# Wide attention of a decoder: causal mask moved from TensorE to VectorE, row sums to ScalarE, and a new order of TensorE's products

## The chip, the cores and the metric

One core of a Trainium2 chip runs the whole kernel as one program. The metric is the time of the program on the device in microseconds (us). Engines are called as the profile calls them: PE is TensorE's matmul, PEld its weight load, DVE is VectorE, ACT is ScalarE, POOL is GpSimd, SP is the queue that issues plain DMAs.

## The reference, cut to what matters

The program is a two-layer decoder on 64 sequences of 64 tokens with 128 channels. Narrow attentions and a mixture of experts come first; the change lies in the self-attention of the second layer, which has 16 heads of 64 dimensions:

```python
def _L1_attn_ref(x, Wq, Wk, Wv, Wo, bo):      # x: layer norm of the residual
    ...
    q = apply_rope(split_heads(x @ Wq))       # x1*cos - x2*sin, x1*sin + x2*cos
    k = apply_rope(split_heads(x @ Wk))
    v = split_heads(x @ Wv)
    sim = jnp.einsum('bid,bjd->bij', q, k) * scale          # scale = 64 ** -0.5
    sim = jnp.where(causal[None], sim, -jnp.inf)
    attn = jax.nn.softmax(sim, axis=-1)
    out = jnp.einsum('bij,bjd->bid', attn, v)
    ...                                       # heads side by side, then @ Wo + bo
```

## The kernel before, in words

The phase `wide_attention_phase` works on 16 blocks of 256 tokens (2 units of 128 rows, 4 sequences) and on 4 groups of 4 heads within each block: 64 items. An item n is a pair of block and group. Every engine has its own program, written as a prologue, a `step` of one block that loops over its 4 groups, and an epilogue; the engines meet at semaphores only, and each takes its instructions strictly in the order in which its program lists them. So that order is the schedule.

In step n PE does, in this order: scores of item n+1 (`scores`, L1540), transposes of the weights of item n (`transpose_e`, L1564), Q of item n+3 (`project_q`), V of item n+1 (`project_v`), K of item n+3 (`project_k`), in the first step of a block the transposes of the next block's input (`transpose_x`), output product of item n-1 (`project_o`), value products of item n (`weigh_values`, L1572). The causal mask is put in by PE: 8 bf16 matmuls (L1552) of an identity with a table of 0 and -1e30 open each bank of scores, and the 64 products of queries and keys (L1560) add to it.

Behind the scores DVE takes the maximum of each row (8 rows of 64 keys on each partition, L1789), subtracts it (L1793), and ACT makes one exponential of all 512 columns (L1674). DVE then adds up the rows (L1799) and takes reciprocals (L1804), POOL multiplies by them (L1440), PE transposes, ACT copies the transposed weights to SBUF (L1681), and PE multiplies with V. Between these, DVE multiplies Q and K by cos and sin (L1765, four operations of 512 columns per item), POOL adds and subtracts them (L1419, L1420), ACT copies V (L1670) and the value products (L1688).

PSUM has 8 banks: V and Q one each (the value products of an item go over both), one that K and the transposed weights share, one for the output, four for the scores. A second kind of work rides along once for each block: DVE adds the experts' rows to the residual (L1737, in the steps of groups 0 and 1), takes statistics (group 2) and centres (group 3), and adds the attention's result (L1810, group 1); ACT normalises (L1645), copies the block's transposed input (L1661) and keeps it (L1654); POOL gathers the experts' rows by DMA (L1456).

Of the kernel before, what the change touches and what calls it, by code (L numbers as in the profile page):

```python
# [7 lines left out]
P = 128  # L8
B, T, C = 64, 64, 128
# [1281 lines left out]
def wide_attention_phase(nc, k):  # L1291
# [11 lines left out]
    with ExitStack() as ctx:  # L1303
# [17 lines left out]
        sin = sb("sin", [P, T])  # L1321
        stats = sb("stats", [P, UB, 6])
# [15 lines left out]
        row_max = sb("row_max", [P, 2, GH * UB])  # L1338
        row_sum = sb("row_sum", [P, 2, GH * UB])
        rsum = sb("rsum", [P, 2, GH * UB])  # L1340

# [6 lines left out]
        KE_ps = ps("KE", [P, 512])  # L1348
# [27 lines left out]
        d_ready = sem("d_ready")  # L1376
        sum_ready = sem("sum_ready")
# [10 lines left out]
        N_WEIGHTS = 7  # L1388
# [15 lines left out]
        @block.sync  # L1404
        def _(sp):
            for dst, name in [(wq, "L1_attn_wq"), (wk, "L1_attn_wk"), (cos, "c_cos"), (sin, "c_sin"), (wv, "L1_attn_wv"),
                              (wo, "L1_attn_wo"), (bias_row, "L1_attn_bo")]:
                sp.dma_start(dst[:], d[name]).then_inc(weights, 16)

        @block.gpsimd  # L1410
        def _(pool):
# [48 lines left out]
            def prologue():  # L1460
# [13 lines left out]
                normalise_e(0, 0)  # L1474
                rotate_k(0, 2)
# [3 lines left out]
            def step(blk, p, prev, nxt):  # L1479
                for g in range(G):  # L1480
                    if later(nxt, 2) and g == 3:
                        power(blk + 2)
                    if g + 1 < G or nxt:
                        normalise_e(*item_at(blk, g + 1))
                    if g + 3 < G or nxt:
                        rotate_q(*item_at(blk, g + 3))
                        rotate_k(*item_at(blk, g + 3))
# [8 lines left out]
        def _(pe):  # L1496
            def transpose_x(nb):

                pe.wait_ge(xn_ready, nb + 1)
                if later(nb, 1):  # L1500
                    pe.wait_ge(d_ready, nb * G - 2)
                for u in range(UB):
                    mm = nc.tensor.transpose(S_ps[:, 0, u * P:(u + 1) * P], xn[:, u, :], k.ident[:])
# [13 lines left out]
            def project_k(blk, g):  # L1517
# [3 lines left out]
                if later(n_, 3):  # L1521
                    pe.wait_ge(et_ready, n_ - 2)
                for a in range(2):
                    mm = nc.tensor.matmul(KE_ps[:, a * TOK:(a + 1) * TOK], wk[:, g, a, :], xnT[:], start=True, stop=True)
# [15 lines left out]
            def scores(blk, g):  # L1540
# [3 lines left out]
                if later(n_, 1):  # L1544
                    pe.wait_ge(d_ready, n_)
# [1158 lines left out]
```

## Time and profile before

| | us |
|---|---|
| median of 3 runs | 1147.18 |
| lowest, highest | 1140.87, 4976.68 |
| profiled execution, its own time | 1146.26 |
| its span | 1144.5 |
| PE busy in the span | 988.8 (86%) |
| DVE busy | 840.3 (73%) |
| POOL busy | 586.9 (51%) |
| ACT busy | 585.6 (51%) |

The span runs from the first to the last instruction on the core. Busy shares are averages over five phases with different limits, so they don't say what bounds one of them. The wide attention lies between 591 and 1009 us of the span.

### The profile page before, as it was taken

Reading aid. Unit: us, or ns where it says so; the run is one execution under the profiler, and the core shown is the slowest. Engines: PE = TensorE matmul, PEld = TensorE weight load, DVE = VectorE, ACT = ScalarE, POOL = GpSimd, SP = SyncE. Lnnn points to the kernel's source line nnn. Section 1 sums busy time; section 2 is a strip of 40 time slices with the busy share of each in tenths; the row PEclk is TensorE's granted clock in tenths of the full one; section 3 lists DMA queues with packets and bytes.
Section 4 is the critical chain, followed back from the end, with each engine's and each line's share of the span. In section 5 each row is a group of like instructions: output and inputs, shape, how many; then the busy total and the mean of one; then the engine's idle time right before and its main releaser. Section 6 shows DMA issues by size and latency. Waiting matters only on the chain. (4 is left out here: it accounts for less than half of the span.)

```text
span 1144.5 us, 38720 instructions
## 1 busy us (share of the span) xinstructions
PE 988.8 (86%) x14758; PEld 800.5 (70%) x14759; DVE 840.3 (73%) x2013; ACT 585.6 (51%) x1014; POOL 586.9 (51%) x735
## 2 busy tenths in 40 slices
PE   5999999999955699999956999999999999868554
PEld 2666666666642699999954888888888888746213
DVE  4878787888839244444426999999999999658696
ACT  3665656677630466666622444444444444446465
POOL 4232424344300433333225888888888886626534
PEclk9999999999965799999987999999999999965585
DMA  8200000100000111111230000000000000041002
GB/s 256 103 2 0 2 11 13 28 20 28 11 28 0 36 48 46 48 48 46 44 111 13 15 13 12 9 11 11 11 9 11 11 11 1 1 112 57 1 1 74
DMA packets 36985, 37.61 MB, mean 33 GB/s; under 512 B 7142, under 2 KB 31145, under 8 KB 36522
## 3 DMA queue, kind: packets, MB, share of 16 engines
q1 hardware_dynamic: 31690, 27.33, 8.0%
q0 software_dynamic: 4352, 8.92, 3.1%
q8 instruction: 48, 0.79, 0.3%
q10 hardware_dynamic: 866, 0.33, 0.1%
q14 instruction: 29, 0.24, 0.1%
HBM read 27.65 MB, written 8.91 MB: 32 GB/s over the span
## 5 line engine op out<-in xcount | busy, mean ns | idle before, releaser
L1283 POOL DMA_INDIRECT e_x<-xn_rows,e_where x72 | 68.4, 950 | 166.5 <-DVE e_where L1264 118.4
L360 POOL TENSOR_SCALAR n_KX<-n_KT,n_of_head 128x512 f32<-128x512 f32 x124 | 84.2, 702 | 121.8 <-ACT n_KT L601 85.0
L1253 DVE COPY e_y<-e_Y_ps 128x128 f32<-128x128 f32 x72 | 21.0, 292 | 112.3 <-PE e_Y_ps L1220 112.3
L760 DVE TENSOR_REDUCE n_row_max<-n_S_ps 128x16 f32<-128x1024 f32 x64 | 78.2, 1221 | 27.0 <-PE n_S_ps L451 27.0
L1440 POOL TENSOR_TENSOR a_E<-a_E,a_rsum 128x512 f32<-128x512 f32 x64 | 66.7, 1042 | 56.2 <-DVE a_rsum L1804 56.2
L665 ACT ACTIVATE n_ET<-n_ET_ps 128x1024 f32<-128x1024 f32 x64 | 65.5, 1024 | 46.4 <-PE n_ET_ps L461 45.6
L461 PEld LDWEIGHTS n_ET_ps<-ident,n_E 128*128 128x128 f32 x512 | 57.1, 142 | 34.9 <-issue 20.1
L764 DVE TENSOR_TENSOR n_E<-n_S_ps,n_row_max 128x1024 f32<-128x1024 f32 x64 | 78.4, 1225 | 2.9
L1210 PE MATMUL e_G_ps<-e_xT,e_gate_here 128*128 128x128 f32 x576 | 78.2, 280 | 0.5 <-ACT e_up_here L1173 0.5
L1220 PE MATMUL e_Y_ps<-m_down_w,e_hT 128*128 x576 | 76.3, 275 | 1.6 <-issue 1.4
L1688 ACT ACTIVATE a_OT<-a_VQ_ps 128x512 f32<-128x512 f32 x64 | 38.2, 598 | 77.0 <-PE a_VQ_ps L1584 77.0
L1210 PE MATMUL e_U_ps<-e_xT,e_up_here 128*128 128x128 f32 x576 | 77.5, 278 | 0.0
L461 PE MATMUL n_ET_ps<-ident,n_E 128*128 128x128 f32 x512 | 68.3, 276 | 8.1 <-ACT n_E L657 8.1
L657 ACT ACTIVATE n_E<-n_E 128x1024 f32<-128x1024 f32 x64 | 67.3, 1052 | 14.3 <-DVE n_E L764 14.2
L1210 PEld LDWEIGHTS e_G_ps<-e_xT,e_gate_here 128*128 128x128 f32 x576 | 72.0, 196 | 0.7 <-ACT e_up_here L1173 0.7
L1184 ACT ACTIVATE e_silu<-e_G_ps 128x512 f32<-128x512 f32 x72 | 43.0, 597 | 57.5 <-PE e_G_ps L1210 51.0
L474 PEld LDWEIGHTS n_PV_ps<-n_VB,n_ET 128*64 128x64 f32 x2048 | 64.9, 138 | 10.5 <-issue 10.5
L1674 ACT ACTIVATE a_E<-a_E 128x512 f32<-128x512 f32 x64 | 40.2, 629 | 61.4 <-DVE a_E L1793 61.4
L1210 PEld LDWEIGHTS e_U_ps<-e_xT,e_up_here 128*128 128x128 f32 x576 | 71.6, 195 | 0.0
L1220 PEld LDWEIGHTS e_Y_ps<-m_down_w,e_hT 128*128 128x128 f32 x576 | 70.2, 192 | 1.9 <-issue 1.9
L474 PE MATMUL n_PV_ps<-n_VB,n_ET 128*64 128x18 f32 x2048 | 71.3, 212 | 0.0
L1456 POOL DMA_INDIRECT a_expert_rows<-slot_out,a_where x64 | 63.6, 994 | 12.1 <-issue 6.7
(282 smaller groups left out, 2686.8 us busy)
## 6 DMA issues: line engine op xcount, KB each, us to landing
slot_out<-e_y SPq DMA_DIRECT2D x72, 64.0 KB
X<-in_x SPq DMA_DIRECT2D x8, 256.0 KB, 5.3
n_ctxT<-in_ctxT SPq DMA_DIRECT2D x8, 256.0 KB, 3.1
m_gate_w<-in_L_ffn_gate_w SPq DMA_DIRECT2D x1, 2048.0 KB, 7.9
m_up_w<-in_L_ffn_up_w SPq DMA_DIRECT2D x1, 2048.0 KB, 13.7
m_down_w<-in_L_ffn_down_w SPq DMA_DIRECT2D x1, 2048.0 KB, 18.0
xn_rows<-n_xn SPq DMA_DIRECT2D x8, 256.0 KB
t_ctxT<-in_ctxT SPq DMA_DIRECT2D x8, 256.0 KB
```

What stands on the lines that cost most here:

```text
L360: last = nc.gpsimd.tensor_scalar(KX[:, p, :, h * T:(h + 1) * T], src, of_head[:, h:h + 1], 1.0, ALU.mult, ALU.mult)
L461: mm = nc.tensor.transpose(ET_ps[:, j * P:(j + 1) * P], E[:, u % 2, j * P:(j + 1) * P], k.ident[:])
L474: mm = nc.tensor.matmul(PV_ps[64 * b:64 * b + 64, j * VW:(j + 1) * VW], ET[:, u % 2, j * P + b * T:j * P + (b + 1) * T], VB[:, p, (2 * u + ...
L657: nc.scalar.activation(E[:, u % 2, :], E[:, u % 2, :], ACT.Exp, scale=1.0 if is_cross(blk) else float(D0) ** -0.5).then_inc(e_ready, 1)
L665: nc.scalar.activation(ET[:, u % 2, :], ET_ps[:], ACT.Copy).then_inc(et_ready, 1)
L760: nc.vector.tensor_reduce(row_max[:, u % 2, :], src, AX.X, ALU.max).then_inc(max_done, 1)
L764: nc.vector.tensor_tensor(E[:, u % 2, :].rearrange("p (j t) -> p j t", t=T), src, row_max[:, u % 2, :].unsqueeze(2).broadcast_to([P, H, T] ...
L1210: mm = nc.tensor.matmul(out[:, c * P:(c + 1) * P], w[:, p, c * P:(c + 1) * P], xT[:, p, :], start=True, stop=True)
L1220: mm = nc.tensor.matmul(Y_ps[p][:, 0:C], hT[:, p, c * P:(c + 1) * P], down_w[:, bass.ds(e * F + c * C, C)], start=(c == 0), stop=(c == FC ...
L1283: nc.gpsimd.indirect_dma_start(out=x[:, j, :], out_offset=None, in_=k.xn_rows, in_offset=bass.IndirectOffsetOnAxis(ap=where[:, j, :], axis ...
L1440: nc.gpsimd.tensor_tensor(e, e, rsum[:, g % 2, :].unsqueeze(2).broadcast_to([P, GH * UB, T]), ALU.mult)\
L1456: nc.gpsimd.indirect_dma_start(out=expert_rows[:, p, i, u, :], out_offset=None, in_=k.slot_out, in_offset=bass.IndirectOffsetOnAxis(ap=whe ...
```

## The change

The constant `c_causal_keys` is no longer multiplied in by PE. A new constant `c_future` (128x128, 0 or -1e30) is loaded by an eighth DMA on SP, before that of wv. One DVE instruction scales the scores, adds this table and writes them to SBUF (`mask_scores`); the maximum is then taken from SBUF with its sign turned. ACT makes eight exponentials of 64 columns for an item, each with its own bias (the negative maximum) and its own sum (`accum_out`), in three portions between its copies. The sum over rows on DVE and the subtraction go.

The transposed weights leave K's bank and go to the first bank of the scores, the transposed input to the second. PE's order in step n becomes: scores n+1, Q n+3, V n+1, transposed weights n, K n+3, transposed input, value products n, output product n-1. DVE starts a step with the reciprocals of item n, where it had those of item n+1 later in the step; POOL divides item n in step n, where it did item n+1, and rotates K of item n+2 before Q of item n+3. In ACT's step exponentials of head 0 and the copy of V come ahead of the copy of the transposed weights. The diff, without declarations and the prologues of DVE, POOL and ACT (whose pieces move in the same sense):

```diff
-            for dst, name in [(wq, "L1_attn_wq"), (wk, "L1_attn_wk"), (cos, "c_cos"), (sin, "c_sin"), (wv, "L1_attn_wv"),
+            for dst, name in [(wq, "L1_attn_wq"), (wk, "L1_attn_wk"), (cos, "c_cos"), (sin, "c_sin"), (future, "c_future"),
+                              (wv, "L1_attn_wv"),
...
-                    if g + 1 < G or nxt:
-                        normalise_e(*item_at(blk, g + 1))
+                    normalise_e(blk, g)
+                    if g + 2 < G or nxt:
+                        rotate_k(*item_at(blk, g + 2))
                     if g + 3 < G or nxt:
                         rotate_q(*item_at(blk, g + 3))
-                        rotate_k(*item_at(blk, g + 3))
                     if nxt == 3:
...
-                if later(n_, 3):
-                    pe.wait_ge(et_ready, n_ - 2)
                 for a in range(2):
-                    mm = nc.tensor.matmul(KE_ps[:, a * TOK:(a + 1) * TOK], wk[:, g, a, :], xnT[:], start=True, stop=True)
+                    mm = nc.tensor.matmul(K_ps[:, a * TOK:(a + 1) * TOK], wk[:, g, a, :], xnT[:], start=True, stop=True)
...
-                    pe.wait_ge(d_ready, n_)
+                    pe.wait_ge(masked, n_)
+                if later(n_, 2):
+                    pe.wait_ge(et_ready, n_ - 1)
...
-                for h in range(GH):
-                    half = slice(64 * (h % 2), 64 * (h % 2) + 64)
-                    for b in range(2):
-                        nc.tensor.matmul(S_ps[64 * b:64 * b + 64, h, 0:P], k.causal_queries[half, 0:T], k.causal_keys[half, 0:P],
-                                         start=True, stop=False)
...
-                                                      RK[rows, g % 2, a, tok], start=False, stop=(a == 1 and u == UB - 1))
+                                                      RK[rows, g % 2, a, tok], start=(a == 0 and u == 0),
+                                                      stop=(a == 1 and u == UB - 1), skip_group_check=True)
                 mm.then_inc(s_ps, 1)
...
-                pe.wait_ge(pk_ready, at_most_all(n_ + 3))
+                pe.wait_ge(masked, at_most_all(n_ + 2))
                 pe.wait_ge(en_ready, n_ + 1)
                 for h in range(GH):
-                    mm = nc.tensor.transpose(KE_ps[:, h * P:(h + 1) * P], E[:, g % 2, h * P:(h + 1) * P], k.ident[:])
+                    mm = nc.tensor.transpose(S_ps[:, 0, h * P:(h + 1) * P], E[:, g % 2, h * P:(h + 1) * P], k.ident[:])
...
                     if g + 1 < G or nxt:
                         scores(*item_at(blk, g + 1))
-                    transpose_e(blk, g)
                     if g + 3 < G or nxt:
                         project_q(*item_at(blk, g + 3))
                     if g + 1 < G or nxt:
                         project_v(*item_at(blk, g + 1))
+                    transpose_e(blk, g)
                     if g + 3 < G or nxt:
                         project_k(*item_at(blk, g + 3))
                     if nxt and g == 0:
                         transpose_x(blk + 1)
+                    weigh_values(blk, g)
                     if g > 0:
                         project_o(blk, g - 1)
                     elif prev:
                         project_o(blk - 1, G - 1)
-                    weigh_values(blk, g)
...
-            def exponentials(blk, g):
-                act.wait_ge(d_ready, blk * G + g + 1)
-                nc.scalar.activation(E[:, g % 2, :], E[:, g % 2, :], ACT.Exp, scale=SCALE).then_inc(e_ready, 1)
+            def exponentials(blk, g, heads):
+                n_ = blk * G + g
+                act.wait_ge(max_ready, n_ + 1)
+                if later(n_, 2):
+                    act.wait_ge(rsum_ready, n_ - 1)
+                for j in range(heads[0] * UB, (heads[-1] + 1) * UB):
+                    e = E[:, g % 2, j * T:(j + 1) * T]
+                    last = nc.scalar.activation(e, e, ACT.Exp, bias=low[:, g % 2, j:j + 1], accum_out=row_sum[:, g % 2, j:j + 1])
+                if heads[-1] == GH - 1:
+                    last.then_inc(e_ready, 1)
 
             def evacuate_e(blk, g):
                 n_ = blk * G + g
                 act.wait_ge(et_ps, n_ + 1)
                 if later(n_, 2):
                     act.wait_ge(pv_ps, n_ - 1)
-                nc.scalar.activation(ET[:, g % 2, :], KE_ps[:], ACT.Copy).then_inc(et_ready, 1)
+                nc.scalar.activation(ET[:, g % 2, :], S_ps[:, 0, :], ACT.Copy).then_inc(et_ready, 1)
...
+                    if g + 1 < G or nxt:
+                        exponentials(*item_at(blk, g + 1), range(1))
+                        evacuate_v(*item_at(blk, g + 1))
                     evacuate_e(blk, g)
                     if g + 1 < G or nxt:
-                        exponentials(*item_at(blk, g + 1))
-                    if g + 1 < G or nxt:
-                        evacuate_v(*item_at(blk, g + 1))
+                        exponentials(*item_at(blk, g + 1), range(1, 2))
+                    if nxt and g == 0:
+                        evacuate_xT(blk + 1)
                     if nxt and g == 2:
                         keep_xT(blk + 1)
-                    if nxt and g == 0:
-                        evacuate_xT(blk + 1)
+                    if g + 1 < G or nxt:
+                        exponentials(*item_at(blk, g + 1), range(2, GH))
...
-            def subtract_max(blk, g):
-
+                products(K_ps[:], PK).then_inc(pk_ready, 1)
+
+            def mask_scores(blk, g):
                 n_ = blk * G + g
                 dve.wait_ge(s_ps, n_ + 1)
-                src = S_ps[:, :, 0:P].rearrange("p h (u t) -> p h u t", t=T)
-                top = row_max[:, g % 2, :].rearrange("p (h u) -> p h u", u=UB)
-                nc.vector.tensor_reduce(top, src, AX.X, ALU.max).then_inc(max_ready, 1)
                 if later(n_, 2):
                     dve.wait_ge(et_ps, n_ - 1)
-                dve.wait_ge(max_ready, n_ + 1)
-                nc.vector.tensor_tensor(E[:, g % 2, :].rearrange("p (h u t) -> p h u t", u=UB, t=T), src,
-                                        top.unsqueeze(3).broadcast_to([P, GH, UB, T]), ALU.subtract).then_inc(d_ready, 1)
+                e = E[:, g % 2, :].rearrange("p (j t) -> p j t", t=T)
+                nc.vector.scalar_tensor_tensor(out=E[:, g % 2, :].rearrange("p (h k) -> p h k", h=GH), in0=S_ps[:, :, 0:P],
+                                               scalar=SCALE, in1=future[:].unsqueeze(1).broadcast_to([P, GH, P]),
+                                               op0=ALU.mult, op1=ALU.add).then_inc(masked, 1)
+                if later(n_, 2):
+                    dve.wait_ge(e_ready, n_ - 1)
+                dve.wait_ge(masked, n_ + 1)
+                nc.vector.tensor_reduce(low[:, g % 2, :], e, AX.X, ALU.max, negate=True).then_inc(max_ready, 1)
 
             def reciprocals(blk, g):
                 n_ = blk * G + g
                 dve.wait_ge(e_ready, n_ + 1)
-                nc.vector.tensor_reduce(row_sum[:, g % 2, :], E[:, g % 2, :].rearrange("p (j t) -> p j t", t=T), AX.X, ALU.add)\
-                    .then_inc(sum_ready, 1)
                 if later(n_, 2):
                     dve.wait_ge(en_ready, n_ - 1)
-                dve.wait_ge(sum_ready, n_ + 1)
                 nc.vector.reciprocal(rsum[:, g % 2, :], row_sum[:, g % 2, :]).then_inc(rsum_ready, 1)
...
+                    reciprocals(blk, g)
                     if g + 1 < G or nxt:
-                        subtract_max(*item_at(blk, g + 1))
+                        mask_scores(*item_at(blk, g + 1))
                     if prev and g == 1:
                         add_residual(blk - 1)
                     if g + 3 < G or nxt:
                         products_q(*item_at(blk, g + 3))
-                    if g + 1 < G or nxt:
-                        reciprocals(*item_at(blk, g + 1))
-                    if g + 3 < G or nxt:
                         products_k(*item_at(blk, g + 3))
```

## Rows read from the trace of the kernel before

**Rows 1.** Windows: stretch; busy (instructions) PE, PEld, DVE, ACT, POOL; clock, DMA, GB/s:

```profile
800.00:825.00 25.00, 24.40 (x581) 21.40 (x571) 23.97 (x45) 11.10 (x22) 21.81 (x28) 1.00 0.04 10
```

**Rows 2.** Timeline of PE (start us, length us), the scores of items 3 and 57:

```profile
635.75 0.30 PE L1560 MATMUL a_S_ps<-a_RK,a_RQ 32*64 32x64 f32 x7
...
962.27 0.28 PE L1560 MATMUL a_S_ps<-a_RK,a_RQ 32*64 32x64 f32 x4
```

**Rows 3.** Timeline of PE, an input transpose; one whole step late in the phase:

```profile
821.86 0.38 PE L1503 MATMUL a_S_ps<-ident,a_xn 128*128 128x128 f32 x2
...
968.15 0.91 PE L1560 MATMUL a_S_ps<-a_RK,a_RQ 32*64 32x64 f32 x64
968.99 0.66 PE L1569 MATMUL a_KE_ps<-ident,a_E 128*128 128x128 f32 x4
969.48 1.03 PE L1514 MATMUL a_VQ_ps<-a_xnT,a_wq 128*128 128x256 f32 x4
...
971.21 1.03 PE L1524 MATMUL a_KE_ps<-a_xnT,a_wk 128*128 128x256 f32 x4
972.08 1.05 PE L1596 MATMUL a_Y_ps<-a_wo,a_OT 128*128 128x128 f32 x8
973.06 0.69 PE L1584 MATMUL a_VQ_ps<-a_ET,a_V 64*64 64x64 f32 x32
973.57 0.29 PE L1552 MATMUL a_S_ps<-causal_keys,causal_queries 64*64 64x128 bf16 x8
973.80 0.91 PE L1560 MATMUL a_S_ps<-a_RK,a_RQ 32*64 32x64 f32 x64
```

**Rows 4.** Timeline, DVE and ACT behind the scores of 968.15:

```profile
969.10 0.69 DVE L1789 TENSOR_REDUCE a_row_max<-a_S_ps 128x8 f32<-128x512 f32 x1 [0.79 <-PE a_S_ps L1560]
...
969.89 0.69 DVE L1793 TENSOR_TENSOR a_E<-a_S_ps,a_row_max 128x512 f32<-128x512 f32 x1
...
970.62 0.63 ACT L1674 ACTIVATE a_E<-a_E 128x512 f32<-128x512 f32 x1 [0.34 <-DVE a_E L1793]
```

**Rows 5.** Timeline of DVE in two steady steps:

```profile
806.20 1.59 DVE L1737 SCALAR_TENSOR_TENSOR X<-a_expert_rows,gates,X 128x128 f32 x2
807.71 0.68 DVE L1789 TENSOR_REDUCE a_row_max<-a_S_ps 128x8 f32<-128x512 f32 x1
...
810.31 0.68 DVE L1799 TENSOR_REDUCE a_row_sum<-a_E 128x8 f32<-128x512 f32 x1
811.08 0.20 DVE L1804 RECIPROCAL a_rsum<-a_row_sum 128x8 f32<-128x8 f32 x1
811.20 0.67 DVE L1765 TENSOR_TENSOR a_PK<-a_KE_ps,a_cos 128x512 f32<-128x512 f32 x1
...
812.39 0.48 DVE L1745 BATCH_NORM_STATS2 a_stats<-X 128x6 f32 x2
...
813.72 0.68 DVE L1789 TENSOR_REDUCE a_row_max<-a_S_ps 128x8 f32<-128x512 f32 x1
```

**Rows 6.** Groups of DVE instructions (xcount | busy us, mean ns | idle before), tail phase:

```profile
L2474 DVE SCALAR_TENSOR_TENSOR t_HT<-t_ET_ps,t_gu_scale,t_act_g 128x512 f32<-128x512 f32 x8 | 5.9, 741 | 3.2 <-ACT t_act_g L2297 3.2
```

**Rows 7.** Timeline of ACT in the tail phase: exponentials of 128x64 with a sum:

```profile
1025.05 0.30 ACT L2257 ACTIVATE t_E<-t_S_ps,t_low 128x64 f32<-128x64 f32 x1
...
1025.34 0.31 ACT L2257 ACTIVATE t_E<-t_S_ps,t_low 128x64 f32<-128x64 f32 x1
```

**Rows 8.** Timeline of ACT, copy of V and the next one:

```profile
809.76 0.58 ACT L1670 ACTIVATE a_V<-a_VQ_ps 128x512 f32<-128x512 f32 x1
810.24 0.41 ACT L1654 ACTIVATE a_xnT_v<-a_xnT 128x256 f32<-128x256 f32 x1
```

**Rows 9.** Timeline, last item: its maxima and its division by the sums:

```profile
999.46 0.69 DVE L1789 TENSOR_REDUCE a_row_max<-a_S_ps 128x8 f32<-128x512 f32 x1 [3.34 <-PE a_S_ps L1560]
...
1002.71 1.04 POOL L1440 TENSOR_TENSOR a_E<-a_E,a_rsum 128x512 f32<-128x512 f32 x1 [4.79 <-DVE a_rsum L1804]
```

**Rows 10.** Timeline of DVE, the first instruction of the phase:

```profile
599.65 0.61 DVE L1737 SCALAR_TENSOR_TENSOR X<-a_expert_rows,gates,X 128x128 f32<-128x128 f32 x2 [11.41 <-DMA a_expert_rows<-slot_out,a_where]
```

More of the change, by code:

```diff
@@ L1321, in wide_attention_phase @@
         sin = sb("sin", [P, T])
+        future = sb("future", [P, P])
         stats = sb("stats", [P, UB, 6])
@@ L1337, in wide_attention_phase @@
         V = sb("V", [P, 2, 2, GH * D1])
-        row_max = sb("row_max", [P, 2, GH * UB])
         row_sum = sb("row_sum", [P, 2, GH * UB])
         rsum = sb("rsum", [P, 2, GH * UB])
+        low = sb("low", [P, 2, GH * UB])
         E = sb("E", [P, 2, GH * P])
@@ L1347, in wide_attention_phase @@
         Q_ps = VQ_ps[:, 1, :]
-        KE_ps = ps("KE", [P, 512])
+        K_ps = ps("K", [P, 512])
         Y_ps = ps("Y", [P, 512])
@@ L1375, in wide_attention_phase @@
         max_ready = sem("max_ready")
-        d_ready = sem("d_ready")
-        sum_ready = sem("sum_ready")
+        masked = sem("masked")
         e_ready = sem("e_ready")
@@ L1387, in wide_attention_phase @@
         passed = sem("passed")
-        N_WEIGHTS = 7
+        N_WEIGHTS = 8
         block = ctx.enter_context(nc.Block())
@@ L1473, in prologue @@
                 rotate_q(0, 2)
-                normalise_e(0, 0)
-                rotate_k(0, 2)
                 for j in range(2 * UB):
@@ L1500, in transpose_x @@
                 if later(nb, 1):
-                    pe.wait_ge(d_ready, nb * G - 2)
+                    pe.wait_ge(masked, nb * G - 2)
                 for u in range(UB):
-                    mm = nc.tensor.transpose(S_ps[:, 0, u * P:(u + 1) * P], xn[:, u, :], k.ident[:])
+                    mm = nc.tensor.transpose(S_ps[:, 1, u * P:(u + 1) * P], xn[:, u, :], k.ident[:])
                 mm.then_inc(xnT_ps, 1)
@@ L1603, in prologue @@
                 transpose_x(0)
-                for g in range(3):
-                    project_q(0, g)
-                    if g == 0:
-                        project_v(0, 0)
-                    project_k(0, g)
-                    if g == 1:
-                        scores(0, 0)
+                project_q(0, 0)
+                project_k(0, 0)
+                project_v(0, 0)
+                project_q(0, 1)
+                project_k(0, 1)
+                scores(0, 0)
+                project_q(0, 2)
+                project_k(0, 2)
             def step(blk, prev, nxt):
@@ L1661, in evacuate_xT @@
                 nc.scalar.activation(xnT[:].rearrange("c (b u t) -> c u b t", b=2, u=UB),
-                                     S_ps[:, 0, 0:TOK].rearrange("c (u b t) -> c u b t", u=UB, b=2), ACT.Copy)\
+                                     S_ps[:, 1, 0:TOK].rearrange("c (u b t) -> c u b t", u=UB, b=2), ACT.Copy)\
                     .then_inc(xnT_ready, 1)
@@ L1705, in prologue @@
                 evacuate_v(0, 0)
-                exponentials(0, 0)
+                exponentials(0, 0, range(GH))
                 normalise(1)
@@ L1822, in prologue @@
                 products_k(0, 1)
+                mask_scores(0, 0)
                 for i in range(2):
@@ L1825, in prologue @@
                 statistics(1)
-                subtract_max(0, 0)
                 products_q(0, 2)
-                reciprocals(0, 0)
                 products_k(0, 2)
@@ L2645, in constants @@
         "c_causal_keys": np.tile(np.where(t[None, :] > t[:, None], NEG, 0.0), (2, 8)).astype(np.float32),
+        "c_future": np.tile(np.where(t[None, :] > t[:, None], NEG, 0.0), (2, 2)).astype(np.float32),
         "c_cos": np.tile(np.cos(angle), (4, 1)).astype(np.float32),
```

1 line of the change is left out of this document (removed).

## The prediction

> **What bounds the kernel now.** I read first the busy time by stretches, then the timeline of one step, then what each engine waits for. In a steady stretch of the wide attention DVE is busy 23.97 of 25 us and PE 24.40, at a granted clock of 1.00, while ACT has 11.10 and POOL 21.81 [rows 1]. Both leaders look full, so the question is which one is waiting. Item 3's scores start at 635.75 and item 57's at 962.27 [rows 2]: 326.52 us for 54 items, 6.05 each, 24.19 for a block of four. Late in the phase, where DVE has no experts' rows to add any more, PE takes 5.65 for a step, from 968.15 to 973.80, without a gap [rows 3]. Here DVE waits 0.79 us for the scores [rows 4]; in the steady stretch it waits for nobody. So PE could run a block in 4 x 5.65 plus at most 0.38 for the input's transposes [rows 3], 22.98, and DVE sets 24.19. The 1.2 us between are DVE's. The wide attention bounds itself; the phases around it are not touched.
>
> **The change part by part.** All lengths are steps from one start to the next, in us.
>
> PE. The causal products go: 973.57 to 973.80, 0.23 [rows 3]. The other pieces stay: scores up to the transposes 0.84, transposes 0.49, Q and V together 1.73 (969.48 to 971.21), K 0.87, output 0.98, values 0.51. Sum 5.42. In the new order, counted from the start of the scores: Q at 0.84, V at 1.71, transposed weights 2.57, K 3.06, values 3.93, output 4.44, next scores 5.42. A block of PE alone is 4 x 5.42 + 0.38 = 22.06.
>
> DVE. The sum over rows goes, 0.77 (810.31 to 811.08) [rows 5]. The maximum with its dependent successor took 0.79 (969.10 to 969.89) [rows 4]; the mask followed by the maximum is the same pair in the other order. The mask's own length isn't in the trace with this form. Its lower end is 0.69, the subtraction it replaces [rows 4]; its upper end 0.74, a three-operand instruction of 128x512 from PSUM that also reads a scalar for each partition [rows 6]. I take 0.69, since the mask's scalar is a constant; 0.05 more would add 0.05 to each loop below. DVE loses 3.1 per block and no longer sets the pace by its sum alone.
>
> ACT. One exponential (0.63, [rows 4]) becomes eight of 64 columns with a bias and a sum. The tail phase has exactly that shape: 1025.05 to 1025.34, 0.29 with the reading of the sum inside [rows 7]. Here the source is SBUF, not PSUM. I take 0.30. The upper end is 0.33: an activation from SBUF took 0.63 and a copy of the same size from PSUM 0.58 [rows 4, 8], which is 0.05 for fixed cost, most of it in the shade of its predecessor. The lower end is 0.29. Eight make 2.4 where 0.5 stood; With 4.2 items in 25 us ACT goes from 11.1 to about 11.1 + 4.2 x 1.9 = 19 and isn't full, but its order matters now.
>
> The Trainium skill, "ScalarE: Activation LUTs", section "What ACT_TABLE_LOAD costs", speaks against this part: an activation with a bias from memory costs about 280 ns plus 0.833 ns a column, which is 333 ns for 64, above the 300 of the tail's row. By it each of the eight would cost 0.03 more, and the sum below would come out near the time before, 1145.
>
> **The new loop.** The value products of item n wait for ACT's copy of the transposed weights. Before, Q, V, K and the output lay between transposes and value products; now K alone does, 0.87, and ACT has the first two exponentials of item n+1 and the copy of V ahead of that copy. Those exponentials wait for DVE. So the step is a chain: scores start, mask starts D later (0.95 at best, 968.15 to 969.10 [rows 3, 4]), maximum 0.79, exponential 0.73 (969.89 to 970.62 [rows 4]), two exponentials 0.60, copy of V 0.48 (809.76 to 810.24 [rows 8]), copy of the weights 0.58 (as long as V's) and 0.06 to reach PE, values 0.51, output 0.98, next scores. Length D + 4.73, at best 5.68, which is 0.26 longer than PE's own 5.42.
>
> D in turn depends on DVE: K's product is complete at 3.06 + 1.03 + 0.04 = 4.13, cos and sin take 1.19 (811.20 to 812.39), then the block's extra work, then the reciprocals 0.12. That gives D = 5.44 + extra + s - previous length, with extra 1.51 for the experts' rows (806.20 to 807.71) and 1.33 for statistics (812.39 to 813.72) [rows 5]; s is PE's delay at Q, which now waits for ACT's copy of the value products. That copy ends D + 5.52 after the scores (4 exponentials' worth more behind the weights' copy), or 0.30 later in steps with a copy of the block's input (0.41 long, [rows 8]); Q needs it at 0.84 of the next step. The four steps:
>
> - group 0: D 0.95; PE's own 5.42 + 0.38 = 5.80 is longer than the chain: 5.80.
> - group 1: D = 5.44 + 1.51 - 5.80 = 1.15, chain 5.88; s = 0.95 + 5.82 - 5.80 - 0.84 = 0.13.
> - group 2: D = 5.44 + 0.13 + 1.51 - 5.88 = 1.20, chain 5.93.
> - group 3: D = 0.95 (5.44 + 1.33 - 5.93 is less); s = 1.20 + 5.82 - 5.93 - 0.84 = 0.25; chain 5.68, PE 5.67.
>
> Sum 23.29. I add 0.2 for short waits that no chain here holds (an estimate: PE idles 0.6 in 25 us, [rows 1]): 23.5 a block. Against 24.19 that is 0.7 less, for 54 items or 13.5 blocks 9.3.
>
> POOL. Its work is the same, now dividing item n in step n. The reciprocals start at D - 0.12 and are 0.20 long [rows 5], the division is 1.04 long [rows 9], and with 0.1 to pass between engines it is ready at D + 1.2, 2.2 to 2.4; PE asks at 2.57: free, with 0.2 to spare. Rotating K first costs nothing, its products are from the step before. If this cover goes (in the step after the one where POOL also adds the bias), it costs up to 0.2 a block.
>
> Edges. The last six items ran at PE's 5.65 or a little above; the chain gives 5.68: nothing. Behind the last scores the way from maximum to division was 3.25 (999.46 to 1002.71 [rows 9]); now 0.79 + 0.73 + eight exponentials 2.4 + two copies 0.96 + 0.10 + 0.35 = 5.3: plus 2.1, less 0.23 for the mask. In the prologue K comes before V and gathers now precede the first division; I set it at nothing, between -2 and +1. The extra DMA of SP stands among seven others that are issued while DVE waits 11.41 for the experts' rows [rows 10]: nothing, and if all of wv, wo and bias came later by its time, under 1.
>
> Sum: 1146.26 (the profiled execution, span 1144.5) - 9.3 + 1.9 = 1138.9, **1139**. The median of the runs, 1147.18, lies 0.9 above it, so the sum against it would read 1140.
>
> **The rivals.**
>
> Rival 1, PE is the bound after all: 5.42 a step plus 0.38 a block, 5.52. It needs the exponentials and copies to hide, that is, a chain shorter by 0.3 to 0.5. For it: DVE is freed of 3.1 per block, PE is busy 24.40 of 25 already. Against: the chain above. 54 x 0.53 = 28.6, plus 6 x 0.23 = 1.4 at the end, less 1.9: **1118**.
>
> Rival 2, slower: the eight exponentials fill ACT's order. If each takes 0.40, the value products' copy ends 0.8 later, Q waits 0.2 to 0.85 in each step, K and DVE's products of K follow, and the next mask too. The same four lines with 0.40 give 6.05, 6.12, 6.48 and 6.27, 24.9, with the 0.2 25.1: 0.9 x 13.5 = 12.2 more, and 2.7 at the end, **1161**. It decides from about 0.34 an exponential; at 0.33 the lines give 23.8 + 0.2 and 1145. At 0.50 the time would pass 1170. Against it: rows 7.
>
> Rival 3, no gain: the chain is as sized but POOL (21.81 of 25 busy, [rows 1]) is late with divisions by 0.2 to 0.3 in each step, since it starts them only after the reciprocals of the same step; K, D and the chain shift: 1143 to 1148.
>
> **How the numbers follow.** The forecast's case 0.45, rival 1 0.20, rival 2 0.17 (half of it beyond 2%), rival 3 0.18. About 2% is what a measurement of this kernel can tell from no change: below 1124 or above 1170. Faster by over 2%: rival 1 and a little of the forecast's lower side, 0.22. Slower: 0.08. Within: 0.70. The range goes from 1117 (rival 1) to 1156, which leaves out the upper half of rival 2 and a faster prologue under rival 1. The likeliest case's own range is 1131 to 1146.
>
> **What would show it.** Right: in a steady block PE waits before the value products for the copy of the weights, 0.2 to 0.5 a step; a block takes 23.3 to 23.7; DVE waits for scores and for K; an exponential steps by 0.30. Rival 1: PE without gaps, 5.42 a step. Rival 2: PE waits at Q for the copy of the value products. Rival 3: PE waits at the transposes for POOL. The forecast is wrong if the mask is over 0.8 long, or if the copies on ACT find it idle.

## The result: slower by 1.3 per cent, and the profile after

The changed kernel takes 1158.64 us (median of 4 runs, 1154.88 to 1159.37) beside 1146.21 for the kernel before on the same chip: ratio 1.0127, 95% interval 1.0099 to 1.0154. One of the four executions of the kernel before took 4976.68 us; the ratio uses the undisturbed ones alone and so isn't the quotient of the two medians. The forecast was 1139, with a range from 1117 to 1156: the direction was wrong, and the time lies outside the range.

The busy time of the whole span, from the page:

```profile
PE 994.9 (86%) x14244; PEld 792.9 (68%) x14247; DVE 773.3 (67%) x1949; ACT 706.4 (61%) x1974; POOL 585.1 (51%) x735
```

DVE has lost 67 us and ACT gained 121, as intended, and yet the time rose. The steady stretch, to be read against [rows 1] (columns as there):

```profile
800.00:825.00 25.00, 23.87 (x485) 20.13 (x484) 18.53 (x39) 18.46 (x83) 20.95 (x27) 1.00 0.04 10
```

DVE is relieved (18.53 where 23.97 stood), ACT is at 18.46 as forecast (19), PE is less busy (23.87, before 24.40). No engine is full now, PE the least idle with 1.1 us of 25: a sign of a chain over several engines. PE's timeline of one step and the starts of the next scores, to be read against [rows 3]:

```profile
802.47 0.91 PE L1554 MATMUL a_S_ps<-a_RK,a_RQ 32*64 32x64 f32 x64
803.31 1.13 PE L1513 MATMUL a_VQ_ps<-a_xnT,a_wq 128*128 128x256 f32 x4
804.28 1.03 PE L1534 MATMUL a_VQ_ps<-a_wv,a_xnT_v 128*128 128x256 f32 x4
805.14 0.60 PE L1564 MATMUL a_S_ps<-ident,a_E 128*128 128x128 f32 x4
805.58 1.03 PE L1521 MATMUL a_K_ps<-a_xnT,a_wk 128*128 128x256 f32 x4
806.91 0.69 PE L1579 MATMUL a_VQ_ps<-a_ET,a_V 64*64 64x64 f32 x32 [0.30 <-ACT a_ET L1684]
807.54 1.16 PE L1591 MATMUL a_Y_ps<-a_wo,a_OT 128*128 128x128 f32 x8
808.63 0.91 PE L1554 MATMUL a_S_ps<-a_RK,a_RQ 32*64 32x64 f32 x64
...
814.78 0.91 PE L1554 MATMUL a_S_ps<-a_RK,a_RQ 32*64 32x64 f32 x64
...
821.11 0.91 PE L1554 MATMUL a_S_ps<-a_RK,a_RQ 32*64 32x64 f32 x64
...
827.27 0.91 PE L1554 MATMUL a_S_ps<-a_RK,a_RQ 32*64 32x64 f32 x64
```

The steps last 6.16, 6.15, 6.33 and 6.16, 24.80 for this block; a block of the kernel before took 24.19. The other engines in the first of these steps:

```profile
803.42 0.69 DVE L1795 SCALAR_TENSOR_TENSOR a_E<-a_S_ps,a_future 128x512 f32<-128x512 f32 x1 [0.42 <-PE a_S_ps L1554]
...
804.22 0.69 DVE L1801 TENSOR_REDUCE a_low<-a_E 128x8 f32<-128x512 f32 x1
...
804.94 0.35 ACT L1675 ACTIVATE a_E<-a_E,a_low 128x64 f32<-128x64 f32 x1 [1.69 <-DVE a_low L1801]
...
805.28 0.33 ACT L1675 ACTIVATE a_E<-a_E,a_low 128x64 f32<-128x64 f32 x1
...
805.62 0.57 ACT L1666 ACTIVATE a_V<-a_VQ_ps 128x512 f32<-128x512 f32 x1
...
806.09 0.58 ACT L1684 ACTIVATE a_ET<-a_S_ps 128x512 f32<-128x512 f32 x1
```

Read as one chain: scores 802.47, mask 803.42, maximum 804.22, first exponential 804.94, copy of V 805.62, copy of the weights 806.09, value products 806.91, output 807.54, next scores 808.63. Every link starts when the one ahead allows it. What the engines wait for between 660 and 950 us (total us, times, longest) says the same for all steps:

```profile
ACT a_E L1675 <- DVE a_low L1801: 76.9, 47, 2.0
...
DVE a_E L1795 <- PE a_S_ps L1554: 26.1, 47, 0.7
...
PE a_VQ_ps L1579 <- ACT a_ET L1684: 11.5, 35, 0.4
```

DVE waits for scores in each of 47 steps, ACT for the maximum in each, PE for the copied weights in 35 of 47. The other 12 are the steps in which the input's transposes fill the gap; there PE's own work is 6.16 long.

**Where the 13.1 us of the profiled spans went** (starts of scores; the last column runs from item 63's scores to the last addition to the residual):

| kernel | item 3's scores | a block, items 3 to 57 | items 57 to 63 | item 63 to end |
|---|---|---|---|---|
| before | 635.75 | 24.19 | 34.43 | 11.33 |
| after | 635.29 | 24.77 | 36.74 | 14.50 |

0.58 x 13.5 blocks = 7.9, the last six steps 2.3, the end 3.2, the prologue -0.5: 12.9. The rest of the span is equal within 0.2.

The end has a cause of its own. PE in the last steps, and the windows of that stretch:

```profile
1004.75 0.69 PE L1579 MATMUL a_VQ_ps<-a_ET,a_V 64*64 64x64 f32 x32 [1.94 <-ACT a_ET L1684]
...
1010.81 0.98 PE L1579 MATMUL a_VQ_ps<-a_ET,a_V 64*64 64x64 f32 x32 [1.94 <-ACT a_ET L1684]
...
1016.02 1.13 PE L1579 MATMUL a_VQ_ps<-a_ET,a_V 64*64 64x64 f32 x32 [0.78 <-ACT a_ET L1684]
1017.08 3.78 PE L1591 MATMUL a_Y_ps<-a_wo,a_OT 128*128 128x128 f32 x16
```

```profile
1006.00:1010.80 4.80, 2.88 (x77) 2.29 (x77) 1.58 (x3) 2.94 (x12) 1.04 (x1) 1.00 0.01 3
1014.00:1021.00 7.00, 5.92 (x52) 5.17 (x52) 0.04 (x1) 1.20 (x2) 0.01 (x1) 0.50 0.01 2
```

Behind two waits of 1.94 us for the copied weights the granted clock falls from 1.00 to 0.50, that is from 2.4 to 1.2 GHz, and the last 16 output products take 3.78 us. With four exponentials (a7 below), where these two waits are 1.66 and 1.67, the clock stays up; the last value and output products are then:

```profile
995.74 0.69 PE L1579 MATMUL a_VQ_ps<-a_ET,a_V 64*64 64x64 f32 x32 [1.67 <-ACT a_ET L1684]
...
999.62 0.69 PE L1579 MATMUL a_VQ_ps<-a_ET,a_V 64*64 64x64 f32 x32 [0.78 <-ACT a_ET L1684]
1000.24 2.05 PE L1591 MATMUL a_Y_ps<-a_wo,a_OT 128*128 128x128 f32 x16
```

16 products in 2.05. From the start of item 63's reciprocals to the addition to the residual it is 5.63 us there (996.77 to 1002.40), 5.60 in the kernel before (1002.43 to 1008.03) and 8.29 here (1012.68 to 1020.97). So about 2.7 us of the 13 go with the slower clock at the very end. The long waits for the copied weights aren't the only way to it: in a3 and a1 below PE waits 2.21 and 2.64 us for POOL at the last transposes, and the output products behind take 3.76 us for 16 and 1.92 for 8.

### The profile page after: what moved, and what is told of

Same layout as the page of the kernel before. It is cut to its first block and busy times, and to the rows that moved or that the text cites. A ratio compares the mean times of both kernels' runs of the same rounds, so it can differ in the third digit from the quotient of the medians.

```text
span 1157.6 us, 38810 instructions
## 1 busy us (share of the span) xinstructions
PE 994.9 (86%) x14244; PEld 792.9 (68%) x14247; DVE 773.3 (67%) x1949; ACT 706.4 (61%) x1974; POOL 585.1 (51%) x735
## 5 line engine op out<-in xcount | busy, mean ns | idle before, releaser
L1675 ACT ACTIVATE a_E<-a_E,a_low 128x64 f32<-128x64 f32 x512 | 171.6, 340 | 104.8 <-DVE a_low L1801 104.8
L1675 ACT ACTIVATION_READ_ACCUMULATOR a_E<-a_E,a_low 128x1 f32 x512 | 98.5, 192 | 0.0
L1591 PE MATMUL a_Y_ps<-a_wo,a_OT 128*128 128x128 f32 x512 | 76.5, 295 | 0.0
L1513 PE MATMUL a_VQ_ps<-a_xnT,a_wq 128*128 128x256 f32 x256 | 72.3, 405 | 4.6 <-DVE a_PQ L1771 2.6
L1172 ACT ACTIVATE e_gate_here<-m_gate_w 128x512 f32 x72 | 45.4, 631 | 46.6 <-PE e_U_ps L1210 24.0
```

Of the source, the lines that this page charges most:

```text
L1513: mm = nc.tensor.matmul(Q_ps[:, a * TOK:(a + 1) * TOK], wq[:, g, a, :], xnT[:], start=True, stop=True)
L1591: mm = nc.tensor.matmul(Y_ps[:, u * P:(u + 1) * P], OT[:, g % 2, u, j, :], wo[:, g, j, :], start=(g == 0 and u == 0 and j == 0), stop=(g = ...
L1675: last = nc.scalar.activation(e, e, ACT.Exp, bias=low[:, g % 2, j:j + 1], accum_out=row_sum[:, g % 2, j:j + 1])
```

## Experiments

The ratio is to the kernel before, run beside each (1142.0 to 1143.6), with its 95% interval; the changed kernel's is 1.0127. The block is read from the trace, as in the table above.

| run | us | ratio | block |
|---|---|---|---|
| a1 output first | 1147.92 | 1.0030 [1.0016, 1.0045] | 24.20 |
| a2 wait order | 1150.00 | 1.0058 [1.0038, 1.0077] | 24.25 |
| a3 exponentials behind | 1175.86 | 1.0274 [1.0242, 1.0307] | 26.00 |
| a5 = a1 + a2 | 1146.75 | 1.0034 [1.0019, 1.0050] | 24.13 |
| a6 = a5, copy on DVE | 1148.14 | 1.0037 [1.0022, 1.0052] | 24.28 |
| a7 four exponentials | 1140.88 | 0.9975 [0.9959, 0.9991] | 23.86 |
| c1 = a5 + a7 | 1138.52 | 0.9965 [0.9951, 0.9979] | 23.67 |
| k5 sums on DVE | 1151.27 | 1.0068 [1.0042, 1.0094] | 24.38 |
| k4 = k5 + a5 | 1141.36 | 0.9992 [0.9978, 1.0005] | 23.81 |
| k1 = k4, one exponential | 1136.40 | 0.9942 [0.9920, 0.9964] | 23.84 |
| b1 before, output behind | 1155.75 | 1.0107 [1.0078, 1.0136] | 24.99 |
| b2 before, no causal products | 1138.53 | 0.9956 [0.9944, 0.9969] | 24.10 |

**a1: the output product ahead of the value products** (the order of before), all else as changed.

```diff
+                    (project_o of the item before)
                     weigh_values(blk, g)
-                    (project_o of the item before)
```

> The changed kernel with one part undone: TensorE's output product goes back ahead of the value products. Theory A (the step is a chain through ScalarE: scores, mask, maximum, two exponentials, copy of V, copy of the transposed weights, value products, output, next scores, 6.16 us in the trace of the changed kernel): the copy then hides behind K and the output product, the wait before the value products goes, and the step becomes 5.5 to 5.7, held by the copy of the value products that Q waits for. About 1158.6 - 0.45 x 56 = 1133, between 1130 and 1143. Theory B (ScalarE is simply too full with eight exponentials): no change, 1155 to 1160. Theory C (TensorE's own instructions have become longer next to one another, 1.16 for an output group instead of 1.05 and a value group that holds 0.62 instead of 0.51): output groups go back to 1.05, and that alone would give 0.2 a step, 1146.

Measured 1147.92: 10.7 us back, not 25 (the block gives 0.57 x 13.5 = 7.7 of them, the last six steps 2.4). PE's timeline:

```profile
803.93 0.69 PE L1579 MATMUL a_VQ_ps<-a_ET,a_V 64*64 64x64 f32 x32
804.56 1.01 PE L1554 MATMUL a_S_ps<-a_RK,a_RQ 32*64 32x64 f32 x64
...
810.42 0.92 PE L1554 MATMUL a_S_ps<-a_RK,a_RQ 32*64 32x64 f32 x64
811.77 1.10 PE L1513 MATMUL a_VQ_ps<-a_xnT,a_wq 128*128 128x256 f32 x4 [0.42 <-ACT a_OT L1691]
...
816.82 1.12 PE L1554 MATMUL a_S_ps<-a_RK,a_RQ 32*64 32x64 f32 x64 [0.27 <-issue]
817.91 1.10 PE L1513 MATMUL a_VQ_ps<-a_xnT,a_wq 128*128 128x256 f32 x4
```

The value products no longer wait: the chain through the copied weights is real and was the limit. But now Q waits for ACT's copy of the value products, up to 0.42, a link forecast as rival 2's. Another part isn't on any other engine: once a block PE waits 0.27 with nothing that the profile shows, and the group of scores then takes 1.09 until Q starts instead of 0.84.

**a2: the wait for the copied weights last.** In the changed kernel PE waits first for these, then for V, then for DVE's products of Q, with a counter after them.

```diff
-                pe.wait_ge(et_ready, n_ + 1)
                 pe.wait_ge(v_ready, at_most_all(n_ + 2))
-                wait_here(pe, pq_ready, at_most_all(n_ + 4), passed)
+                pe.wait_ge(pq_ready, at_most_all(n_ + 4))
+                wait_here(pe, et_ready, n_ + 1, passed)
```

> The changed kernel with the same three waits before the value products in another order: the copy of the transposed weights, which comes last, is waited for last. In the trace the value products start 0.24 us after that copy ends; two more waits and a counter stand behind the one for it. Theory A with the waits as a link of the chain: 0.10 to 0.18 less a step, 1148 to 1153. If the 0.24 is the passing between engines alone: no change, 1157 to 1160.

1150.00, as expected: waits that had long been satisfied, standing behind the late one, cost 8.6 us in all. From the end of the copy to PE it was 0.24 a step (806.67 to 806.91) and is 0.10 (813.72 to 813.82).

**a3: both copies ahead of the first exponentials.**

```diff
-                        exponentials(*item_at(blk, g + 1), range(1))
                         evacuate_v(*item_at(blk, g + 1))
                     evacuate_e(blk, g)
+                        exponentials(*item_at(blk, g + 1), range(1))
```

> The changed kernel with ScalarE's first two exponentials moved behind the copies of V and of the transposed weights. The value products then wait for nothing that VectorE does. Theory A in its simple form (only that chain counts): 5.9 a step, 1143. Theory A with the second chain (exponentials end later, the copy of the value products behind them too, and Q waits for that copy): about 6.3 a step with a wait of 0.4 at Q, 1158 to 1168. Theory B (ScalarE too full): no change, as its work is the same.

1175.86, slower than either figure. The wait is the second chain's, but larger than I put it, 0.5 in each of 45 steps:

```profile
PE a_VQ_ps L1513 <- ACT a_OT L1691: 22.3, 45, 0.7
```

A block of 26.00 is 0.31 a step longer than the changed kernel's. The trace holds the loop behind this wait:

```profile
811.71 1.13 PE L1513 MATMUL a_VQ_ps<-a_xnT,a_wq 128*128 128x256 f32 x4 [0.52 <-ACT a_OT L1691]
...
818.08 1.10 PE L1513 MATMUL a_VQ_ps<-a_xnT,a_wq 128*128 128x256 f32 x4 [0.40 <-ACT a_OT L1691]
```

```profile
813.74 0.60 ACT L1666 ACTIVATE a_V<-a_VQ_ps 128x512 f32<-128x512 f32 x1 [2.08 <-PE a_VQ_ps L1534]
...
817.36 0.58 ACT L1691 ACTIVATE a_OT<-a_VQ_ps 128x512 f32<-128x512 f32 x1
```

Q at 811.71, V at 812.67, ACT's copy of V at 813.74 and of the weights at 814.23, all eight exponentials from 814.71 to 817.36 (2.65), the copy of the value products, and Q again at 818.08: 6.37. DVE isn't in this loop, but all eight exponentials are, and it is longer than the 6.16 of the chain that the edit cut.

**a5: a1 and a2 together.**

> Both edits together: output product ahead of the value products, and the copy of the transposed weights waited for last. With the output product ahead the value products no longer wait for the copy, so the order of the waits should be worth little: 1145 to 1149, like the first edit alone (1148). If the waits cost TensorE time even when all of them are long fulfilled, 0.05 to 0.1 a step less: 1142 to 1145.

As expected, no more than a1 alone: with the output in between the copied weights aren't late.

**a6: a5, and the copy of the value products as DVE's last piece of a step** (`nc.vector.tensor_copy` in place of ACT's).

> The same two edits, and the copy of the value products moved from ScalarE (behind six exponentials) to the end of VectorE's step. Theory A (after the first edit the pace is held by that copy, for which Q waits 0.1 to 0.4 a step): the wait at Q goes, a step is 5.6 to 5.8 (TensorE's own pieces in the trace of the first edit add up to 5.58), 1125 to 1138. If the pace is held by GpSimd or VectorE behind it: no gain or a loss, 1143 to 1155, as VectorE gets 0.6 more a step and the mask comes later.

1148.14, the second of the two figures: in the step with statistics Q waits for DVE in place of ACT.

```profile
810.77 1.10 PE L1513 MATMUL a_VQ_ps<-a_xnT,a_wq 128*128 128x256 f32 x4 [0.58 <-DVE a_OT L1814]
```

**a7: four exponentials of 128 columns.**

```diff
-                for j in range(heads[0] * UB, (heads[-1] + 1) * UB):
-                    e = E[:, g % 2, j * T:(j + 1) * T]
+                for j in range(heads[0] * UB, (heads[-1] + 1) * UB, UB):
+                    e = E[:, g % 2, j * T:(j + UB) * T]
```

> The changed kernel with four exponentials of 128 columns in place of eight of 64, one for each head; the maximum and the sum of the second unit of a head are left out (the first unit's stand for both). One of them ahead of the copies instead of two: 0.39 instead of 0.68 in the chain. Theory A: 0.29 less a step until TensorE's own length with its longer pieces (5.69) is reached, 1140 to 1145. Theory C alone (TensorE's pieces are the whole loss): no change, 1156 to 1160.

1140.88, as expected: 17.8 us less than the changed kernel, and but for DVE's reciprocal (0.17 in place of 0.20) only ACT's work became less. 12.4 of it lie in the blocks, 1.4 in the last six steps and 3.8 behind item 63's scores, 2.7 of these with the clock. It shows how much of the step hangs on ACT's order.

**c1: a5 and a7 together.**

> The changed kernel with all three reliefs of its chain at once: output product ahead of the value products, the wait for the weights' copy last, four exponentials of 128 columns (the second unit's maximum and sum are left out). In the traces so far the blocks of a7, k1 and k4 take 23.86, 23.84 and 23.81 us, whatever was relieved. Theory A (the chain through ScalarE is the only limit over TensorE's own step): now TensorE's own 4 x 5.58 + 0.40 = 22.7 a block is left, 1.1 x 13.5 = 15 less than with four exponentials alone: about 1126, range 1122 to 1131. Theory B (some common limit stands behind it, the slow groups of scores and the order of POOL and VectorE, about 23.8 a block): 1136 to 1142.

1138.52: theory B. Of PE's waits between 660 and 950 us none is for another engine any more, yet the block is 23.67, not 22.7 (theory A):

```profile
805.97 1.05 PE L1554 MATMUL a_S_ps<-a_RK,a_RQ 32*64 32x64 f32 x64
806.94 1.13 PE L1513 MATMUL a_VQ_ps<-a_xnT,a_wq 128*128 128x256 f32 x4
...
812.10 1.12 PE L1554 MATMUL a_S_ps<-a_RK,a_RQ 32*64 32x64 f32 x64 [0.27 <-issue]
813.19 1.10 PE L1513 MATMUL a_VQ_ps<-a_xnT,a_wq 128*128 128x256 f32 x4
```

Scores to Q takes 0.97 and 1.09 where 0.84 was seen, and once a block PE waits 0.27 where the loop starts over. Three kernels with quite different loads on ACT (k1, k4, c1) end here. In the steps of items 58 to 61, where no experts' rows, gathers and statistics run beside any more, all three take 5.58 to 5.60, which is theory A's 5.58: the common limit isn't PE's order alone.

**k5: the sums back on DVE, the changed kernel's order kept**, and **k4: the same with a5's edits.** ACT's exponentials lose the reading of the accumulator.

```diff
-   nc.scalar.activation(e, e, ACT.Exp, bias=low[...], accum_out=row_sum[...])
+   nc.scalar.activation(e, e, ACT.Exp, bias=low[...])
+   nc.vector.tensor_reduce(row_sum[...], E[...], AX.X, ALU.add)   # ahead of the reciprocals
```

> The changed kernel with one part undone: the row sums are taken on VectorE again, and ScalarE's eight exponentials have no sum; TensorE's order stays. Theory A: two exponentials ahead of the copies cost 0.48 instead of 0.68, 0.2 less in the chain, but VectorE starts its mask up to 0.3 to 0.5 later in the steps with extra work, in that same chain: 6.15 to 6.35 a step, 1155 to 1168. Theory B (ScalarE too full): 0.7 less a step, 1120 to 1135.

> The changed kernel with output product ahead of the value products, the copy of the transposed weights waited for last, and the row sums back on VectorE (0.78 at the start of its step); ScalarE keeps eight exponentials, but without a sum each (0.24 instead of 0.33). The result is the exact softmax as before. Theory A: the copy of the value products ends 0.5 earlier and Q no longer waits; VectorE has 4.65 + extras a step, 21.9 a block, below TensorE's 4 x 5.58 + 0.22 + 0.3 = 22.8. A step of 5.75 to 5.85: 1126 to 1133. If VectorE's later mask (0.78 more ahead of it) is the next link: 5.9 to 6.0, 1135 to 1143. If GpSimd, which divides after the sums, is: TensorE waits at the transposes, about the same.

k5 gave 1151.27, 7 less than the changed kernel, between the two figures. Three steps of four take 5.97 to 6.04, the fourth 6.4: behind the statistics DVE's later mask carries through ACT to PE:

```profile
816.51 0.69 PE L1580 MATMUL a_VQ_ps<-a_ET,a_V 64*64 64x64 f32 x32 [0.56 <-ACT a_ET L1685]
```

k4 gave 1141.36, the second figure. ACT's sums thus cost about 6 us more than DVE's in either order of PE (1146.75 to 1141.36 and 1158.64 to 1151.27): the sum over rows that the change took from DVE was worth keeping there.

**k1: k4 with one exponential of 512 columns**, whose bias is the maximum over all 512 columns of a partition.

> As the kernel with the sums on VectorE and the output product ahead, with a single exponential of 512 columns: its bias is the negative maximum over all eight rows of a partition, which is the same softmax as long as no row lies far below. ScalarE then has the load it had before the change. Theory A: with the chain through the value products' copy already hidden, only 0 to 0.1 a step less than with eight exponentials: 1124 to 1133. If it is much faster (below 1120), ScalarE's load was the limit there.

1136.40, the fastest, 0.6% below the kernel before, but above its expectation: the same 23.84 a block.

**b1: the kernel before with the output product behind the value products.**

> The kernel before with one part of the change alone: value products ahead of the output product. Theory C (an output group that follows the 64x64 value products is 0.1 longer, and the value group in front of it holds 0.1 more): in the last steps, where TensorE sets the pace, a step is 5.75 to 5.87 instead of 5.65; in the steady part VectorE sets 6.05 and hides most: 1146 to 1150. Without such a cost: 1146 and 5.65 in the last steps.

1155.75: this order alone, with the causal products, the one exponential and DVE's work of before, costs 12.2 us, as much as the whole change. PE's timeline (steady stretch):

```profile
806.79 0.69 PE L1584 MATMUL a_VQ_ps<-a_ET,a_V 64*64 64x64 f32 x32 [0.16 <-DVE a_PQ L1765]
807.42 1.16 PE L1596 MATMUL a_Y_ps<-a_wo,a_OT 128*128 128x128 f32 x8
808.50 0.31 PE L1552 MATMUL a_S_ps<-causal_keys,causal_queries 64*64 64x128 bf16 x8
808.74 0.91 PE L1560 MATMUL a_S_ps<-a_RK,a_RQ 32*64 32x64 f32 x64
```

Value products to output 0.63, output to the next group 1.08: in [rows 3] the same pieces were 0.51 and 0.98. And with the value products sooner, DVE's products of Q are late for them. Expected were 1146 to 1150. The last steps, expected at 5.75 to 5.87, take 6.15: 0.22 more for the two pieces, and 1.14 in place of 0.86 from K to the value products (979.86 to 981.00), which start 0.24 behind DVE's products of Q (980.76).

**b2: the kernel before without the causal products.**

> The kernel before without TensorE's eight causal products, so without any mask; all else as before. What the removal is worth on TensorE shows in the last steps, where TensorE sets the pace: 5.42 if the products' 0.23 goes whole; 5.53 if the scores behind the 64x64 value products cost 0.1 for the change from one tile size to another, which the causal products of the same size as the value products hid. In the steady part VectorE sets 6.05, so the time stays at 1143 to 1146.

Late steps of PE:

```profile
968.25 0.91 PE L1555 MATMUL a_S_ps<-a_RK,a_RQ 32*64 32x64 f32 x64
...
973.16 0.69 PE L1580 MATMUL a_VQ_ps<-a_ET,a_V 64*64 64x64 f32 x32
973.79 0.91 PE L1555 MATMUL a_S_ps<-a_RK,a_RQ 32*64 32x64 f32 x64
```

A step is 5.54, not 5.42: scores follow the value products after 0.62 where the causal products did after 0.51. 0.12 of the 0.23 is gained, nearly the 5.53 expected. The time lies below the 1143 to 1146 expected: between 660 and 950 DVE holds the block at 24.10, so of the 4.9 us that this kernel is faster only about 1.9 come from the steps (0.09 x 13.5, and 6 x 0.12). Its trace is also without some stalls of PE that no engine causes, ahead of item 3 (631.40, before 635.75) and near the end; no run shows whether the edit removed them.

## Why the prediction was wrong

The mechanism was the one forecast: no engine full, a step set by the chain over scores, mask, maximum, exponentials, copies, value products and output, PE waiting for the copied weights 0.3 a step. That it came slower instead of faster is a matter of this chain's length. **The step that failed is the length of this chain, "D + 4.73, at best 5.68".** It is 6.16 in three steps of four (6.33 in the fourth, see DVE below):

| link | forecast | measured | |
|---|---|---|---|
| scores to mask (D) | 0.95 | 0.95 | |
| mask, maximum, to the exponential | 1.52 | 1.52 | |
| two exponentials | 0.60 | 0.68 | +0.08 |
| copies of V and of the weights | 1.06 | 1.05 | -0.01 |
| copy's end to PE | 0.06 | 0.24 | +0.18 |
| value products | 0.51 | 0.63 | +0.12 |
| output | 0.98 | 1.09 | +0.11 |

Over a block that is 24.77 against 23.5: 1.27 x 13.5 = 17.2 of the 20.4 us between 1139 and the profiled execution's 1159.37. The last six steps (+2.3 against nothing) and the end (+3.2 against +1.9), less 0.5 in the prologue, are the other 3.1. The last six stood at "the chain gives 5.68: nothing" and fell with the same step.

**PE's own step, 5.42.** Wrong, and this hid how small the stake was. Without waits it is 5.69 (6.16 with the input's transposes, 0.47 more and not 0.38): 0.84 scores, 0.97 Q, 0.86 V, 0.44 transposes, 0.86 K, 0.63 values, 1.09 output. Before it was 5.65 [rows 3]. I carried each piece over with its length, but that depends on its neighbours, and each time the neighbour had another tile size: values 0.12 more (b2 and b1 show it alone), output 0.11 (b1: 0.10), Q behind the scores 0.10 (0.97 for 0.87), transposes 0.05 less. So the causal products' 0.23 were paid back in full. Rival 1's 1118 (0.20) was out of reach: with 4 x 5.69 + 0.47 = 23.2 a block the forecast's own sum gives about 1135 even if everything else hides, an estimate from these rows. The Trainium skill, "TensorEngine Tiling (Array Packing)", section "Key Properties", says that a change of the tiling mode drains TensorE; it gives no price. These runs show 0.10 to 0.12 us at three joints, 0.05 at the transposes behind the scores and none at the output ahead of the value products (0.98 in [rows 3] and in a1). That the drain is the cause is argued, since no run changes the tile size alone.

**Exponentials.** 0.33 to 0.34 from one to the next, not 0.30. The tail's row had its source in PSUM [rows 7]; no run shows whether that is the difference. I had named 0.33 as the upper end. The group between 660 and 950 us, and the mask's:

```profile
L1675 ACT ACTIVATE a_E<-a_E,a_low 128x64 f32<-128x64 f32 x372 | 124.7, 341 | 76.9 <-DVE a_low L1801 76.9
...
L1795 DVE SCALAR_TENSOR_TENSOR a_E<-a_S_ps,a_future 128x512 f32<-128x512 f32 x47 | 32.5, 692 | 26.1 <-PE a_S_ps L1554 26.1
```

The Trainium skill, "ScalarE: Activation LUTs", section "What ACT_TABLE_LOAD costs", gives 333 ns for 64 columns, and the trace agrees with 341 on average. But that is the length of one; the same section lets neighbours overlap by about 93 ns, which makes 0.24 from one to the next, and this is what k4 shows without the sums. The prediction set the length against a distance, and it came out near the measured 0.33 only because the reading of the sum adds 0.09. Even at 0.33 the forecast was 1145, still 14 short, since the exponentials are 0.08 of the 0.48 missing.

**From ACT's copy to PE.** I took 0.06, seen where nothing else was waited for. a2 shows that the waits behind the late one made it 0.24: with the late one last it is 0.10.

**DVE.** The mask at 0.69 was right (692 ns), and DVE ceased to be the limit. D was at its best, 0.95, in three steps of four. In the fourth (814.78) the scores hold PE for 0.97 in place of 0.84, the mask starts 1.05 behind them and the first exponential 1.59 behind the mask in place of 1.52: 0.17 more, the 6.33. The 1.51 for the experts' rows became 0.60, so the two steps I had put at D = 1.15 and 1.20 weren't late; this softened the miss by 0.45 a block.

**POOL.** Hidden, as said; rival 3 is out. The division starts at

```profile
803.09 1.04 POOL L1441 TENSOR_TENSOR a_E<-a_E,a_rsum 128x512 f32<-128x512 f32 x1 [0.43 <-DVE a_rsum L1808]
```

and ends 1.0 us before PE asks for it (805.14); in the three steps behind it is 0.4 to 1.3 us.

**Rival 2** gave 1161 and a time on the right side, but by a price of 0.40 that isn't there. Its wait, Q for the copy of the value products, is nearly absent in the changed kernel; it is the next limit once the first chain is cut (a1).

**The end.** +3.2 came out near the +1.9, but of other terms: from item 63's scores to its reciprocals it was 5.7 before (996.70 to 1002.43), 1.5 of it a stall in the middle of the scores that no engine causes and that the changed kernel doesn't have, and it is 6.2 now (1006.47 to 1012.68). 2.0 more for the way through ACT, less that 1.5, plus 2.7 behind the reciprocals, with the clock: 3.2. That PE's longer waits there could bring the clock down wasn't in the forecast at all.

**The range** went to 1156 because I bounded D and the exponentials, and never the joints of PE nor the handoff, four terms taken as known.

## What to carry to other kernels

Moving a piece of PE between pieces of another tile size changed lengths by 0.05 to 0.12 us here; bound each new neighbourhood before counting a gain, above all where the gain is a few tenths of a step. A loop that one full engine holds can turn into one held by a chain over three engines with none full: then every tenth of a link is paid in each step, and the last wait in front of a late instruction should be the late one. When relieving a link, look at the next one first: here taking the output product's 1.09 out of the chain of each step was worth 0.14 (a1).

## What the runs showed of the hardware that was not expected

- The same DVE instruction that adds the experts' rows (two inputs in SBUF) takes 833 ns on average between 660 and 950 us before:

```profile
L1737 DVE SCALAR_TENSOR_TENSOR X<-a_expert_rows,gates,X 128x128 f32 (+1 forms) x48 | 38.2, 833 | 0.0
```

and 349 after:

```profile
L1743 DVE SCALAR_TENSOR_TENSOR X<-a_expert_rows,gates,X 128x128 f32 x44 | 13.5, 349 | 0.0
```

Before, it ran beside POOL's rotations (806.18 to 807.64, [rows 5] for DVE's side); now it runs beside POOL's gather, in one of two cases with its first 0.16 us still beside a rotation. In the kernel before, too, two of them take 0.61 together in [rows 10], where POOL only issues gathers. The Trainium skill, "SBUF — State Buffer", section "SBUF: two separate sides", describes a port pair that a DVE instruction with two inputs in SBUF and a GpSimd instruction that reads SBUF take in turns, each for its whole length; the numbers agree with it.
- Waits that are already satisfied still cost PE: with three waits and a counter from the late release to the matmul it is 0.24 us, with one wait and the counter (a2) 0.10.
- Reading the accumulator is an instruction of 193 ns on ACT, of which about 0.09 us stays in the distance between two exponentials (0.33 with it, 0.24 in k4 without).
- Open: groups of 64 score products sometimes take 1.04 to 1.20 us in place of 0.91, in a1, a6, k1, k4 and c1, while no engine is waited for. With PE's wait of 0.27 where the loop starts over this is about 0.9 us a block and what keeps k1, k4 and c1 at 23.7 to 23.8. In c1 the groups of items 54 to 63 last 0.85 to 0.94 until the next piece. No run here tells its cause.
